# The last sums of a decoder: two row groups of every four go through ScalarE and TensorE, and six groups are requested ahead instead of three

## The reference, cut to what matters

```
logits = einsum('btd,ed->bte', x, router_w)
top_vals, top_idx = top_k(logits, 2)
top_w = softmax(top_vals, axis=-1)
h = square(relu(einsum('nd,edh->enh', xf, w1)))      # all experts
y = einsum('enh,ehd->end', h, w2)
out = w_f[:, 0] * y_sel[:, 0] + w_f[:, 1] * y_sel[:, 1]   # y of the two chosen experts of each row
x = x + out
```

## Time and profile before

| what | value |
|---|---|
| median of 3 runs | 2876.21 us (2872.34 to 2879.39) |
| the profiled execution, its own time | 2876.75 us |
| its span, first to last instruction | 2874.9 us |
| first request for results after the barrier (L2211) | 2827.55 us |
| last sum starts | 2869.49 us |

### The profile page before, as it was taken

How to read it: one execution, slowest core, us unless ns; L and a number is a source line. 1 busy time by engine, 2 the same in 40 slices (tenths; PEclk the granted TensorE clock), 3 DMA queues, 4 the chain that set the end, 5 groups by cost and what they waited for, 6 DMA issues and landing times. The chain is left out here.

```text
span 2874.9 us, 57394 instructions
## 1 busy us (share of the span) xinstructions
PE 2575.8 (90%) x19210; PEld 2037.6 (71%) x19210; DVE 1529.1 (53%) x3357; ACT 1122.1 (39%) x2398; POOL 599.6 (21%) x652
## 2 busy tenths in 40 slices
PE   7999979789999975999999799899799999579992
PEld 4555555478888864888888566566688888468881
DVE  6777756456766664000000288455577777643334
ACT  2333345345555540333333244222455555312220
POOL 0000000023333310222222100000233333125542
PEclk9999999989999987999999899899899999779995
DMA  5110157777777732555555699000588888226666
GB/s 146 45 29 25 29 174 263 273 194 192 186 189 190 188 93 74 192 192 192 192 192 188 191 343 308 29 1 1 136 204 209 204 203 206 73 93 210 206 208 188
DMA packets 288417, 463.56 MB, mean 161 GB/s; under 512 B 75074, under 2 KB 216228, under 8 KB 288276
## 3 DMA queue, kind: packets, MB, share of 16 engines
q1 hardware_dynamic: 271508, 412.45, 50.3%
q0 software_dynamic: 16768, 49.30, 5.3%
HBM read 342.60 MB, written 119.02 MB: 161 GB/s over the span
## 5 line engine op out<-in xcount | busy, mean ns | idle before, releaser
L1444 ACT ACTIVATE x_probT<-banks 125x448 f32<-125x448 f32 x768 | 418.0, 544 | 382.9 <-PE banks L1341 372.8
L1544 DVE TENSOR_REDUCE x_neg_max<-banks 112x2 f32<-112x750 f32 x512 | 455.4, 930 | 93.4 <-PE banks L1325 93.4
L2103 PE MATMUL banks<-f_xT,f_w 128*128 128x256 f32 (+1 forms) x1680 | 369.9, 377 | 21.8 <-DMA f_b<-in_L_ffn_b 8.6
L2103 PEld LDWEIGHTS banks<-f_xT,f_w 128*128 128x128 f32 x1680 | 310.6, 197 | 74.9 <-issue 11.1
L1490 POOL TENSOR_TENSOR x_diag<-ident,x_neg_max 112x448 fp32r<-112x448 f32 x256 | 240.9, 941 | 581.6 <-DVE x_neg_max L1544 550.6
L2115 PE MATMUL banks<-f_w,f_hT 128*128 128x256 f32 x1584 | 355.8, 381 | 0.0
L1339 PE MATMUL banks<-x_diag,x_ones 112*125 112x448 f32 x768 | 324.0, 422 | 0.7 <-ACT x_probT L1444 0.6
L2115 PEld LDWEIGHTS banks<-f_w,f_hT 128*128 128x128 f32 x1584 | 297.7, 192 | 37.6
L1341 PEld LDWEIGHTS banks<-x_qP,x_kP 128*125 128x125 f32 x1536 | 290.5, 189 | 14.9
L1341 PE MATMUL banks<-x_qP,x_kP 128*125 128x224 f32 x1536 | 290.6, 271 | 0.0
L2162 DVE TENSOR_TENSOR f_y<-banks,f_b 128x256 f32<-128x256 f32 x66 | 25.1, 420 | 475.7 <-PE banks L2115 475.7
(11 more groups left out here) (331 smaller groups left out, 3789.1 us busy)
## 6 DMA issues: line engine op xcount, KB each, us to landing
x_kP<-k_halves SPq DMA_DIRECT2D x512, 188.0 KB, 3.6
f_w<-in_L_ffn_w SPq DMA_DIRECT2D x70, 1024.0 KB
f_w<-in_L_ffn_w SPq DMA_DIRECT2D x70, 512.0 KB
x_qP<-q_halves SPq DMA_DIRECT2D x512, 56.0 KB, 3.2
x_v<-v_rows SPq DMA_DIRECT2D x64, 408.0 KB, 3.2
k_halves<-p_halves SPq DMA_DIRECT2D x32, 752.0 KB, 4.5
k_halves<-f_d_halves SPq DMA_DIRECT2D x32, 752.0 KB, 6.4
q_halves<-x_q_halves SPq DMA_DIRECT2D x64, 224.0 KB, 2.3
```

The lines of the kernel that those rows point to most:

```text
L1444: act.activation(probT[:, u % 2, c].rearrange("k h t -> k (h t)"), ST[i % 2][0:KB, 0:HU * T], ACT.Exp).then_inc(exp_done, 1)
L1544: dve.tensor_reduce(mx[:, u % RING, 2 * pair:2 * pair + 2], psum[0:T, 2 * pair:2 * pair + 2, 0:NKV], AX_X, ALU.max, negate=True).then_inc( ...
L2103: last = pe.matmul(bank[1 + f % 3][:, 0:width], w1[:, r, k, f * P:(f + 1) * P], xT[:, r, k, 0:width], start=(k == 0), stop=(k == KD - 1))
```

## The change

In layer 1 alone RING becomes 6, so six groups (twelve transfers) may be requested before any sum is done. Layer 0 keeps 3. Of the four blocks s of each group, s = 0 and 1 are summed as before. For s = 2 and 3 ScalarE multiplies both rows by their weights, in place in `near`; TensorE adds the two by two matmuls with the identity into one bank (start on the first, stop on the second), the banks taken in turn; and VectorE adds the bank to x in one tensor_tensor. A group now counts SUMS = 6 increments of `added` instead of 8, and the waits of SyncE and GpSimd go by that. Two semaphores, `weighed` and `paired`, are new.

```
-        RING = 3
+        RING = 3 if layer == 0 else 6
...
+        weighed, paired = flag("weighed"), flag("paired")
+        MINE = GROUP // 2
+        SUMS = 2 * MINE + GROUP - MINE
...
-                        sp.wait_ge(added, 2 * GROUP * (g + 1))
+                        sp.wait_ge(added, SUMS * (g + 1))
...
+                @block.scalar
+                def _(act):
+                    for g in range(NG):
+                        act.wait_ge(collected[g % RING], 32 * (g // RING + 1))
+                        for s in range(MINE, GROUP):
+                            for c in range(2):
+                                act.activation(near[:, g % RING, c, s, :], near[:, g % RING, c, s, :], ACT.Copy,
+                                               scale=share[:, c, g * GROUP + s:g * GROUP + s + 1]).then_inc(weighed, 1)
+
+                @block.tensor
+                def _(pe):
+                    for g in range(NG):
+                        for s in range(MINE, GROUP):
+                            n = g * (GROUP - MINE) + s - MINE
+                            if n >= len(bank):
+                                m = n - len(bank)
+                                pe.wait_ge(added, SUMS * (m // (GROUP - MINE)) + 2 * MINE + m % (GROUP - MINE) + 1)
+                            for c in range(2):
+                                pe.wait_ge(weighed, 2 * n + c + 1)
+                                last = pe.matmul(bank[n % len(bank)][0:T, 0:D], ident[0:T, 0:T],
+                                                 near[:, g % RING, c, s, :], start=(c == 0), stop=(c == 1))
+                            last.then_inc(paired, 1)
...
-                        pool.wait_ge(added, 2 * GROUP * (g - RING + 1))
+                        pool.wait_ge(added, (2 * GROUP if layer == 0 else SUMS) * (g - RING + 1))
...
+                    if layer == 1 and s >= MINE:
+                        n = g * (GROUP - MINE) + s - MINE
+                        dve.wait_ge(paired, n + 1)
+                        link(dve.tensor_tensor(x[:, b, :], x[:, b, :], bank[n % len(bank)][0:T, 0:D], ALU.add))
+                        continue
                     dve.wait_ge(collected[g % RING], 32 * (g // RING + 1))
```

## The result

The changed kernel took 2866.78 us, the median of 7 runs (2863.16 to 2868.03), against 2875.40 us for the kernel before in 7 runs (2870.73 to 2879.39). The ratio is 0.9971, with a 95% interval of 0.9960 to 0.9983: 8.6 us faster, where no change was forecast and 3.7 us was called the most that any reordering could bring.

What follows compares the result with a forecast made beforehand. The prediction took DMA transfers to bound the closing block. From 2876.75 us, +0.1 for the last arrival and +0.2 for the last group's sums gave 2877.05; less 0.54 to the runs' median, 2876.5 us, range 2870.5 to 2880.5.

Steps and rivals of the forecast that it cites:

- What bounds the kernel now: Closing block, 47.35 us: VectorE (33.2 us) and DMA engines (37 us without a gap) both full, the DMA engines fuller.
- The ring of six: GpSimd's read requests: six groups ahead remove only waits that no transfer felt; last arrival moves by +0.1 us.
- The ceiling of 3.7 us: End of the closing block: the most any reordering can bring, with all 40.1 us of transfers setting the end.
- VectorE: Sums in the closing block: 16.6 us removed, 7.3 us added, so VectorE falls from 33.2 to 23.9 us.
- I take 0: VectorE's saving outside the last group: worth 0, since 1.6 us of each 4.56 us between arrivals becomes idle.
- ScalarE: 32 weighings in place: four take 2.06 us a group on an idle engine and cost nothing by themselves.
- TensorE: 32 matmuls: 1.03 us each at half clock, 0.47 at full clock; last group taken as 4.3 us, 0.2 later.
- the full-clock end of the bounds: Last group, from arrival: the add ends at 3.15 us at full clock, against about 5.25 at half clock.
- VectorE was the rhythm: Rival for the closing block: VectorE's saving of 9.3 us comes out in full, giving 2866.9 us; chance 0.04.
- Reads go first: Rival for the DMA queues: a deep read queue keeps stores back, span ends 3.7 us sooner, 2872.8 us; chance 0.10.
- TensorE's pairs: Rival for the closing block: four matmuls make a group cost 5.6 us, last sum 9.8 us later, 2886 us; chance 0.04.

Runs made afterwards that it cites:

- the ring of six on VectorE: Kernel before with six groups requested ahead in layer 1 and all 64 sums still on VectorE; timed ratio to before 0.9992 (0.9983 to 1.0002).

## Why the prediction was wrong

*What bounds the kernel now.* The counts were right (33.2 us of VectorE, 40.1 us of packet time), the reading of them was not. From the share of 1.00 from 2829 to 2866 I concluded that the DMA engines were at their limit and the reads never dry. A share adds up whatever packets there are. It was kept at 1.00 by a store that ran while reads were missing and then while they waited, ten packets to one. The three waits for results in the earlier trace rows said so, and were read as the sign of a full queue.

*The ring of six* is the step that failed first: "with three groups the queue was never empty while reads remained". At 2839.9 two of the three groups, 1 and 2, were read and not yet fully summed, so one alone was under way; and with its stores left out the kernel before kept its read queue busy for 85.4% of the time. Worth +0.1 us in the sum, the last arrival moved by -7.1 us, and with the ring alone the reads were done at 27.4. The ceiling of 3.7 us, from which the range took its lower end, came from adding the packets' times, 28.4 and 11.7 us; but reads and stores together went at 330 GB/s where the reads alone got 254 to 258. In the changed kernel the reads' own packet time is 63.2% of 41 us, 25.9 us and not 28.4.

*VectorE.* 7.3 and 16.6 us were right (0.420 and 0.485 us measured), and so was "I take 0" for this edit alone: the shared sums without the ring brought nothing. It was wrong for both together, because each covers the other: -3.0 us for the ring, +0.6 for the sums, -7.6 for both, by one profiled execution each. By the timed runs either half alone can't be told from no change, and only both together are clear of it.

*ScalarE* cost less, 0.496 us each and four in 1.71 us instead of 2.06. *TensorE* took 0.90 us a matmul at clock 0.51 in the first group (3.61 us for four), 0.49 at full clock after; it was granted 1.00 from 2837 on. So the last group took 3.1 us from arrival, the full-clock end of the bounds, 1.2 us under the 4.3 that were taken.

*The rivals.* "VectorE was the rhythm" named 2866.9 us, within 0.2 of the median, and its mechanism is not the one that ran: its saving alone gives nothing, and arrivals came 3.5 us apart as it asks, but at a DMA share near 1, which it excludes. That a number fits is no proof of its story. "Reads go first" was right in what it described, stores landing in 11.7 us and a last arrival before 2862, and wrong in its price, which stood on the sum of packet times. TensorE's pairs were not the rhythm of the changed kernel: its VectorE waited 1.8 us in all for banks.

Open is why a request needs 8.7 to 10.7 us to arrive beside stores and 6.5 to 7.6 without them, when the engines alternate packet by packet with a deep queue. The stretch at 2839.4 shows one part of it, a store going ahead whole. The other side of it is as open: the first store moved its first packet 1.5 us after its issue in the kernel before (2838.03, 2839.53) and 5.2 us after it in the changed one (2837.66, 2842.91), where twelve reads had been asked for ahead of it.

## What to carry to other kernels

A busy share of 1 says that the queues hold something, not that they hold what is waited for: split it by queue in short windows, and count how many buffers are really under way, not filled and waiting for their reader. A ring of n buffers needs n x (time of one in the queue) to exceed sums + request + way to arrival under load; here four were enough, and three cost the whole gain. Where two bounds lie within some 10% of each other, as 33.2 and 37 us did here, price the edits together, since each one alone may show nothing.

## What the runs showed of the hardware that was not expected

- Stores and reads overlap: reads alone went at 254 GB/s in the changed kernel and 286 in the ring of six on VectorE, both kinds together at 330 and 372, with the reads at 253 and 291 of them while as many 4 KB read packets as 1 KB store packets moved; stores alone went at 385. With the sizes the other way round the reads had 194 in the mean, and 80 while a store was under way.
- An engine that issued many DMAs on its hardware queue was held in the issue: ScalarE 0.36 to 0.52 us each for the first five, then up to 2.05 us, 20.8 us for 16 transfers of 448 KB, and up to 7.1 us each where GpSimd's queue was reading too. GpSimd on its software queue took 0.71 us each throughout (16 in 11.33 us) and was not held with sixteen requested.
